# Two 8-expert mixtures in a six-stage transformer kernel: tiles of 128 rows, weights kept on chip, each tile's weights copied to a fixed place

## The chip, the cores and the metric

The kernel runs on one core of one Trainium2 chip. The metric is the device time of one launch in microseconds (us); lower is better. The program is written engine by engine: TensorE (PE), VectorE (DVE), ScalarE (ACT), GpSimd (POOL) and SyncE (SP), which only issues DMAs here, each have their own list of instructions, and semaphores order them against each other.

## What is computed

2048 tokens of 128 numbers pass through six stages, each with a residual: a 64-expert mixture, an attention, the 64-expert mixture again, an 8-expert mixture, a second attention, and the 8-expert mixture again. The change touches only the two 8-expert mixtures (called f1 and g1 in the code, their tensors `f_...` and `g_...`):

```python
x = x + 0.5 * _L1_ffn_ref(_layernorm(x, axis=-1), ...)   # stages 4 and 6

def _L1_ffn_ref(x, Wg, bg, W1, b1, W2, b2):      # 8 experts, 128 -> 512 -> 128
    probs = softmax(x @ Wg + bg, axis=-1)
    h = relu(einsum('bsd,edf->bsef', x, W1) + b1)
    all_out = einsum('bsef,efd->bsed', h, W2) + b2
    top_vals, top_idx = top_k(probs, 2)
    weights = top_vals / (sum(top_vals) + 1e-09)
    selected = take_along_axis(all_out, top_idx[..., None], axis=2)
    return sum(selected * weights[..., None], axis=2)
```

## The kernel before

The function `mixture_one` builds one such stage. All data are 32-bit floats. It has a **preamble** and a **tile loop**.

Preamble. VectorE computes the layer norm (L144 to L159), TensorE turns it (L165) and multiplies it by the gate (L369), and VectorE picks the two best experts of each token (L449 to L464) and computes, from ranks that TensorE sums (L376 to L382), the place of each of the 4096 (token, choice) pairs in a list sorted by expert (L469 to L484). In DRAM the list is `slots_dram`: it is cut into tiles of `SLOTS` = 256 rows, each tile of one expert alone, so there are at most `PASSES` = 16 + 7 = 23 tiles, and a row is 132 numbers (the token's vector and its number). SyncE fills the list with empty rows at the stage's start (L302). Once the places are known, GpSimd scatters the rows into it with 32 indirect DMAs (L352). The number of each tile's expert is put into `tile_expert` (L487 to L490).

Weights. SyncE loads them per tile: it reads the tile's expert into a register (`value_load`, L311) and issues four DMAs, W1 (256 KB), b1, W2 (256 KB) and b2 spread over all partitions (L312 to L315), into one of `WBUF` = 6 buffers. Six tiles' weights are loaded during the scatter, the others behind the loop as buffers come free. When all rows are scattered, four DMAs bring the list back to SBUF as `xin` (L321), in groups of tiles (0), (1 to 3), (4 to 11) and (12 to 22).

Tile loop. For tile i TensorE turns its rows (`turn`, L389, two transposes), VectorE copies the result out of PSUM (`xT_out`, L509), TensorE makes the 512 hidden values (`hidden`, L398, four matmuls of 256 columns), ScalarE adds b1 and applies relu (L434, four operations), TensorE multiplies by W2 (`down`, L407, eight matmuls of 128 columns), VectorE adds b2 (`y_out`, L516), and GpSimd scatters the tile's two halves to `back_dram` by token number (L358, two indirect DMAs). TensorE's order is written out by hand:

```python
        turn(0)
        for i in range(PASSES):
            if i + 1 < PASSES:
                turn(i + 1)
            hidden(i)
            if i >= 1:
                down(i - 1)
        down(PASSES - 1)
```

At the end SyncE waits for all of GpSimd's DMAs, loads `back` in four parts (L329), and VectorE adds each token's two rows, times their weights, to x (L531).

Of the kernel before, what the change touches and what calls it, by code (L numbers as in the profile page):

```python
# [22 lines left out]
P = 128  # L23
# [175 lines left out]
def mixture_one(core, name, ctx, w):  # L199

    nc = core.nc
# [28 lines left out]
    fill = sb("fill", [P, E1])  # L232
# [5 lines left out]
    tile_number = sb("tile_number", [1, PASSES])  # L238
    tile_cmp = sb("tile_cmp", [1, PASSES, E1])
    tile_sum = sb("tile_sum", [1, PASSES])  # L240
    tile_expert = sb("tile_expert", [1, PASSES], I32)
    place = sb("place", [P, TILES, E1])
# [10 lines left out]
    w1 = [sb(f"w1_{i}", [P, F1]) for i in range(WBUF)]  # L253
    w2 = [sb(f"w2_{i}", [P, FC1, P]) for i in range(WBUF)]
    b1 = [sb(f"b1_{i}", [P, FC1]) for i in range(WBUF)]
    b2 = [sb(f"b2_{i}", [P, P]) for i in range(WBUF)]
    xin = sb("xin", [P, PASSES * HALVES, ROW])
    xT = sb("xT", [P, 2, SLOTS])
    hT = sb("hT", [P, 2, FC1, SLOTS])
    y = [sb(f"y{i}", [P, HALVES, P]) for i in range(YBUF)]  # L260
# [25 lines left out]
    rows_sent, *y_sent = core.indirect([16 * K * TILES] + [16 * HALVES * len(range(s, PASSES, YBUF)) for s in range(YBUF)])  # L286
    w_loaded = [sem(f"w_loaded{i}") for i in range(WBUF)]
# [9 lines left out]
    def sync(sp):  # L297
# [6 lines left out]
        sp.wait_ge(experts_ready, 1)  # L304

        def weights(i):
            s = i % WBUF
            if i >= WBUF:
                sp.wait_ge(y_ready, i - WBUF + 1)
                sp.wait_ge(relu_done, FC1 * (i - WBUF + 1))  # L310
            e = sp.value_load(tile_expert[0:1, i:i + 1], min_val=0, max_val=E1 - 1)  # L311
            sp.dma_start(w1[s][:, :], w["W1"][ds(e, 1)].rearrange("a d f -> d (a f)")).then_inc(w_loaded[s], 16)  # L312
            sp.dma_start(b1[s][:, :], w["b1"][:, ds(e, 1), :].rearrange("p a c -> p (a c)")).then_inc(w_loaded[s], 16)
            sp.dma_start(w2[s][:, :, :], w["W2"][ds(e, 1)].rearrange("a (c p) d -> p (a c) d", p=P)).then_inc(w_loaded[s], 16)
            sp.dma_start(b2[s][:, :], w["b2"][ds(e, 1), :].to_broadcast([P, P])).then_inc(w_loaded[s], 16)  # L315

        for i in range(WBUF):
            weights(i)
        wait_sent(sp, rows_sent, 16 * K * TILES)
# [1786 lines left out]
```

## Time and profile before

| | us |
|---|---|
| median of 3 runs (1409.33 to 1413.65) | 1412.22 |
| the profiled execution's own time | 1405.89 |
| its span | 1404.2 |
| first 8-expert mixture, layer norm to the last addition to x | 672.5 to 853.4 |
| second 8-expert mixture, the same | 1217.3 to 1396.1 |
| TensorE busy over the span | 1006.7 (72%) |
| VectorE / ScalarE / GpSimd busy | 792.9 / 599.2 / 285.0 |

A span is the time from the first to the last instruction of the profiled execution. "Busy" leaves out register, branch and DMA-issuing instructions. A 32-bit matmul shows as two records on TensorE, a transpose as one, so `L398 PE ... x8` are the four matmuls of one tile. PEclk is the clock that TensorE was granted: 1.00 is 2.4 GHz and 0.50 is 1.2 GHz. The chain of waits is followed back from the last instruction, at each step to what released it.

### The profile page before, as it was taken

The numbers are of one execution on the slowest core, as the hardware profiler recorded it, in microseconds if no ns is written. First come the engines' busy times: TensorE is split into PE (matmuls) and PEld (weight loads), VectorE is DVE, ScalarE is ACT, GpSimd is POOL, SyncE is SP. The second block draws the span as 40 slices with busy tenths as digits, with TensorE's granted clock in tenths as the row PEclk, the third lists the DMA queues.
The fourth block names the chain that finished last, engine by engine and source line by source line (L and its number), as shares of the span: only waits on it lengthen the run. The fifth ranks groups of instructions, "written<-read, shape, count | busy, mean of one in ns | idle before, by whom it ended". The sixth has DMA issues, their size and how long they took to land.

```text
span 1404.2 us, 25630 instructions
## 1 busy us (share of the span) xinstructions
PE 1006.7 (72%) x8027; PEld 749.0 (53%) x8042; DVE 792.9 (56%) x2560; ACT 599.2 (43%) x1392; POOL 285.0 (20%) x321
## 2 busy tenths in 40 slices
PE   3798922488989667989307971789999999613992
PEld 2346822355656344568306971566676767412992
DVE  6766866756666577678501217377777776530222
ACT  3113613445666340147203431277777777411440
POOL 2103062321210030030073541000000000044552
PEclk8799967679999978999558995699999999855996
DMA  7003000000000060030456636855444443355652
GB/s 204 0 0 102 0 13 0 1 1 2 0 0 0 16 160 0 18 85 0 89 153 181 188 87 214 232 151 151 141 116 136 131 118 114 61 136 146 186 164 90
DMA packets 168677, 125.98 MB, mean 90 GB/s; under 512 B 16595, under 2 KB 151531, under 8 KB 168580
## 3 DMA queue, kind: packets, MB, share of 16 engines
q1 hardware_dynamic: 163588, 116.25, 30.7%
q0 software_dynamic: 4992, 8.54, 1.7%
q8 instruction: 48, 0.79, 0.2%
q14 instruction: 49, 0.40, 0.1%
HBM read 85.89 MB, written 40.69 MB: 90 GB/s over the span
## 4 chain that ended last, share of the span: by engine, by line
PE 56%; DVE 23%; issue 8%; ACT 5%; SPq 3%; DMA 2%; POOL 2%; POOLq 0%; DVEq 0%; ACTq 0%; PEld 0%; PEldq 0%
PE psum L398 6%; PE psum L407 6%; PE psum L746 5%; PE psum L831 4%; PE psum L1227 3%; PE psum L194 3%; PE psum L1779 3%; PE psum L1250 2%; PE psum L1791 2%; PE psum L1821 2%; PE psum L1284 2%; PE psum L1286 2%; PE psum L1215 2%; PE psum L1811 2%; PE psum L165 2%
## 5 line engine op out<-in xcount | busy, mean ns | idle before, releaser
L1460 DVE TENSOR_REDUCE a_negmax<-psum 128x2 f32<-128x512 f32 x128 | 88.4, 691 | 66.1 <-PE psum L1227 65.3
L1371 ACT ACTIVATE a_PT<-psum 128x1024 f32<-128x1024 f32 x64 | 65.5, 1024 | 78.0 <-PE psum L1286 78.0
L973 DVE TENSOR_TENSOR g_S<-g_place,g_number 128x512 bf16<-128x512 f32 (+1 forms) x116 | 76.8, 702 | 16.9 <-PEq L741 6.0
L434 ACT ACTIVATE g_hT<-psum,g_b 128x256 f32<-128x256 f32 x92 | 37.4, 471 | 97.8 <-PE psum L398 97.8
L434 ACT ACTIVATE f_hT<-psum,f_b 128x256 f32<-128x256 f32 x92 | 37.4, 471 | 97.5 <-PE psum L398 97.5
L973 DVE TENSOR_TENSOR f_S<-f_place,f_number 128x512 bf16<-128x512 f32 (+1 forms) x100 | 66.2, 704 | 16.3 <-PEq L741 6.1
L1896 ACT ACTIVATE a_pr<-a_L,a_least 128x128 f32<-128x128 f32 x128 | 50.7, 396 | 54.5 <-DVE a_least L1956 54.5
L1356 ACT ACTIVATE a_turned<-psum 128x1024 bf16<-128x1024 bf16 x64 | 64.4, 1021 | 8.4 <-PE psum L1215 8.4
L1227 PE MATMUL psum<-a_turned 128*128 128x256 bf16 x256 | 53.7, 295 | 13.8 <-DVE a_negmax L1460 11.1
L1898 ACT ACTIVATE a_pr<-a_L,a_least 128x256 f32<-128x256 f32 x128 | 63.5, 496 | 0.0
L1284 PE MATMUL psum<-a_turned 128*128 128x256 bf16 x256 | 60.7, 277 | 1.0 <-issue 0.5
L1286 PE MATMUL psum<-a_shift,a_select 128*128 128x256 bf16 x256 | 60.7, 277 | 0.0
L1779 PE MATMUL psum<-a_KT,a_Q 64*128 64x128 f32 (+1 forms) x512 | 59.3, 350 | 1.4 <-DVE a_least L1956 1.4
L1906 ACT ACTIVATE a_PT<-psum 128x384 f32<-128x384 f32 x128 | 55.8, 490 | 1.8 <-PE psum L1791 1.6
L1791 PE MATMUL psum<-ident,a_pr 128*128 128x128 f32 x384 | 53.6, 276 | 2.8 <-DVE a_pr L1717 2.5
L1811 PE MATMUL psum<-a_PT,a_V 128*64 128x256 f32 (+1 forms) x512 | 55.5, 338 | 0.0
L358 POOL DMA_INDIRECT g_back_dram<-g_y,g_xin x46 | 44.7, 972 | 53.1 <-DVE g_y L516 37.1
L358 POOL DMA_INDIRECT f_back_dram<-f_y,f_xin x46 | 44.7, 972 | 52.6 <-DVE f_y L516 37.9
L1956 DVE CUSTOM_DVE_ANT_0 a_L<-psum,a_X 128x256 f32<-128x256 f32 x128 | 53.6, 419 | 0.0
L1811 PEld LDWEIGHTS psum<-a_PT,a_V 128*64 128x64 f32 x512 | 31.0, 136 | 41.0 <-issue 16.8
L180 POOL CAST a_xs_high<-a_xnT 128x256 fp32r<-128x256 f32 x8 | 4.3, 539 | 231.9 <-PE psum L196 220.8
L1215 PE MATMUL psum<-identb,a_stack 128*128 128x128 bf16 x512 | 43.2, 236 | 10.4 <-ACT a_turned L1356 10.4
(472 smaller groups left out, 2749.2 us busy)
## 6 DMA issues: line engine op xcount, KB each, us to landing
a_z<-a_G SPq DMA_DIRECT2D x32, 512.0 KB, 3.9
a_X<-a_z SPq DMA_DIRECT2D x16, 1024.0 KB, 6.7
f_w<-in_W SPq DMA_DIRECT2D x46, 256.0 KB
g_w<-in_W SPq DMA_DIRECT2D x46, 256.0 KB
a_X<-a_z SPq DMA_DIRECT2D x16, 512.0 KB, 4.1
f_wgu<-in_gate_up SPq DMA_DIRECT2D x16, 384.0 KB, 6.5
g_wgu<-in_gate_up SPq DMA_DIRECT2D x16, 384.0 KB, 4.7
a_z<-a_pad SPq DMA_DIRECT2D x6, 1024.0 KB, 10.3
```

Of the source, the lines that this page charges most:

```text
L358: pool.indirect_dma_start(back_dram[:, :], bass.IndirectOffsetOnAxis(ap=xin[:, HALVES * i + a, P:P + 1].bitcast(I32), axis=0), y[i % YBUF] ...
L398: pe.matmul(bank[2 * (i % 2) + c // 2][:, SLOTS * (c % 2):SLOTS * (c % 2) + SLOTS], w1[i % WBUF][:, P * c:P * c + P], xT[:, i % 2, :], sta ...
L407: last = pe.matmul(bank[4 + i % 2][:, P * a:P * a + P], hT[:, i % 2, c, P * a:P * a + P], w2[i % WBUF][:, c, :], start=(c == 0), stop=(c = ...
L434: act.activation(hT[:, i % 2, c, :], bank[2 * (i % 2) + c // 2][:, SLOTS * (c % 2):SLOTS * (c % 2) + SLOTS], ACT.Relu, bias=b1[i % WBUF][: ...
L973: return dve.tensor_tensor(S[:, slot, :].rearrange("p (t e n) -> p t e n", t=1, n=CAPACITY), bcast(place[:, ds(t, 1), CE * k:CE * k + CE], ...
L1227: last = pe.matmul(bank[0][:, SEQ * j:SEQ * j + SEQ], turned[s][0][:, h + j, P * qt:P * qt + P], turned[s][1][:, h + j, :], start=True, st ...
L1284: pe.matmul(out[:, SEQ * j:SEQ * j + SEQ], turned[s][1][:, h, P * kt:P * kt + P], turned[s][0][:, h, :], start=True, stop=False, skip_grou ...
L1286: last = pe.matmul(out[:, SEQ * j:SEQ * j + SEQ], select[:, h, :], shift[s][:, :], start=False, stop=True, skip_group_check=True)
L1460: dve.tensor_reduce(negmax[:, qt, h:h + 2], bank[0].rearrange("p (h n) -> p h n", n=SEQ), AX.X, ALU.max, negate=True).then_inc(max_done, 1)
L1779: last = pe.matmul(out, Q[s][rows, c, queries], KT[s][rows, c, keys], start=True, stop=True)
L1791: last = pe.transpose(bank[2 + i][:, P * j:P * j + P], pr[:, n % SLOTS, P * j:P * j + P], core.ident[:, :])
L1811: last = pe.matmul(o[D1 * i:D1 * i + D1, queries], V[s][:, kt, D1 * h:D1 * h + D1], PT[:, (2 * m + i) % TSLOTS, keys], start=(kt == 0), st ...
```

## The change

Tiles have 128 rows (`SLOTS = P`), so there are 32 + 7 = 39 of them. All experts' W1 and W2 are loaded once, at the stage's start, right behind the empty rows, into `w12`; before each tile VectorE copies the tile's 128x1024 weights, at an address in a register, into one of three fixed places `wt` (`take_weights`). The 39 registers are loaded by VectorE ahead of the loop. b1 is picked for all tiles ahead of the loop (`tile_bias`), and b2 is no longer added to y: TensorE multiplies the tokens' expert weights `ex` by b2 ahead of the loop, and VectorE adds the product to x. In front of the loop TensorE also does 18 matmuls of 512 columns whose result nobody reads (`WARM`), once 28 of the 32 scatters have landed. The first two tiles' rows now come in one DMA. The diff, cut to its core (both mixtures run this code):

```diff
-    SLOTS = 256
-    HALVES = SLOTS // P
+    SLOTS = P
     PASSES = K * TOKENS // SLOTS + E1 - 1
-    WBUF = 6
-    YBUF = 4
-    GROUPS = ((0, 1), (1, 4), (4, 12), (12, PASSES))
+    YBUF = 6
+    WBUF = 3
+    GROUPS = ((0, 2), (2, 8), (8, 22), (22, PASSES))
+    LAST = 4
+    WARM = 18
...
     def sync(sp):
...
-        sp.wait_ge(experts_ready, 1)
-        def weights(i):
...
-        for i in range(WBUF):
-            weights(i)
-        wait_sent(sp, rows_sent, 16 * K * TILES)
+        sp.dma_start(b1[:, :, :], w["b1"]).then_inc(w_loaded, 16)
+        sp.dma_start(b2[:, :], w["b2"]).then_inc(w_loaded, 16)
+        for e in range(E1):
+            sp.dma_start(w12[:, e, 0:F1], w["W1"][e]).then_inc(w_loaded, 16)
+            sp.dma_start(w12[:, e, F1:2 * F1].rearrange("p (c d) -> p c d", d=P),
+                         w["W2"][e].rearrange("(c p) d -> p c d", p=P)).then_inc(w_loaded, 16)
+        wait_sent(sp, rows_sent, 16 * (K * TILES - LAST))
+        wait_sent(sp, last_sent, 16 * LAST)
...
     def gpsimd(pool):
...
         for i in range(PASSES):
             pool.wait_ge(y_ready, i + 1)
-            for a in range(HALVES):
-                pool.indirect_dma_start(back_dram[:, :],
...
+            pool.indirect_dma_start(back_dram[:, :],
...
     def tensor(pe):
...
+        pe.wait_ge(weights_ready, 1)
+        for t in range(TILES):
+            last = pe.transpose(bank[t // 4][0:E1, P * (t % 4):P * (t % 4) + P], ex[:, t, :], core.ident[:, :])
...
+        pe.wait_ge(w_loaded, 16 * (2 + 2 * E1))
+        for q in range(4):
+            pe.wait_ge(exT_ready, q + 1)
+            for t in range(4 * q, 4 * q + 4):
+                last = pe.matmul(bank[q][:, P * (t % 4):P * (t % 4) + P], exT[:, P * t:P * t + P], b2[:, :], start=True,
+                                 stop=True)
+            last.then_inc(b2_done, 1)
+        wait_sent(pe, rows_sent, 16 * (K * TILES - LAST))
+        for i in range(WARM):
+            pe.matmul(bank[4], core.ones[:, :], sel_flat, start=True, stop=True)
...
         def hidden(i):
-            pe.wait_ge(w_loaded[i % WBUF], 64 * (i // WBUF + 1))
             pe.wait_ge(xT_ready, i + 1)
+            pe.wait_ge(copied, i + 1)
...
         def down(i):
             if i >= 2:
                 pe.wait_ge(y_ready, i - 1)
-            pe.wait_ge(relu_done, FC1 * (i + 1))
-            for a in range(HALVES):
-                for c in range(FC1):
...
+            for c in range(FC1):
+                pe.wait_ge(relu_done, FC1 * i + c + 1)
...
     def vector(dve):
...
+        dve.wait_ge(w_loaded, 16 * (2 + 2 * E1))
+        for c in range(FC1):
+            step(dve.tensor_tensor(tile_pick[:, :, :], tile_cmp[:, :, :],
+                                   b1[:, :, c].unsqueeze(1).to_broadcast([P, PASSES, E1]), ALU.mult))
+            ins = dve.tensor_reduce(tile_bias[:, c, :], tile_pick[:, :, :], AX.X, ALU.add)
...
+        for q in range(4):
+            dve.wait_ge(b2_done, q + 1)
+            xq = core.x[:, 4 * q:4 * q + 4, :]
+            dve.tensor_tensor(xq, xq, bank[q].rearrange("p (t d) -> p t d", d=P), ALU.add).then_inc(b2_added, 1)
+        dve.wait_ge(experts_ready, 1)
+        expert = [dve.value_load(tile_expert[0:1, i:i + 1], min_val=0, max_val=E1 - 1) for i in range(PASSES)]
...
+        def take_weights(i):
+            if i >= WBUF:
+                dve.wait_ge(y_done, i - WBUF + 1)
+            dve.tensor_copy(wt[i % WBUF][:, :], w12[:, ds(expert[i], 1), :].rearrange("p a n -> p (a n)")).then_inc(copied, 1)
+        for i in range(WBUF):
+            take_weights(i)
         xT_out(0)
         for i in range(PASSES):
             if i + 1 < PASSES:
                 xT_out(i + 1)
+            if i >= 1 and i - 1 + WBUF < PASSES:
+                take_weights(i - 1 + WBUF)
             if i >= 1:
                 y_out(i - 1)
```

How the instructions stand before and after, at the places that matter most. TensorE in the tile loop of the first of the two mixtures, before (two tiles; `f_w_0` is a weight buffer, `f_xin` the rows, `f_xT` and `f_hT` the turned rows and the hidden values):

```order
L389 MATMUL psum<-ident,f_xin 128x128 x2
L398 MATMUL psum<-f_xT,f_w_1 128x256 x4
L407 MATMUL psum<-f_w_0,f_hT 128x128 x8
L389 MATMUL psum<-ident,f_xin 128x128 x2
L398 MATMUL psum<-f_xT,f_w_2 128x256 x4
```

and the same place in the changed kernel:

```order
L411 MATMUL psum<-f_sel,ones 128x512 x18
L417 MATMUL psum<-ident,f_xin 128x128 x2
L427 MATMUL psum<-f_xT,f_wt 128x128 x4
L417 MATMUL psum<-ident,f_xin 128x128
L427 MATMUL psum<-f_xT,f_wt 128x128 x4
L436 MATMUL psum<-f_wt,f_hT 128x128 x4
```

The 18 matmuls stand in front of the loop; a tile now has one transpose, four hidden matmuls of half the columns and four output matmuls in place of eight. VectorE in the same loop before:

```order
L503 TENSOR_REDUCE f_weight<-f_part 128x16
L509 COPY f_xT<-psum 128x256 x3
L516 TENSOR_TENSOR f_y<-psum,f_b_0 128x256
L509 COPY f_xT<-psum 128x256
L516 TENSOR_TENSOR f_y<-psum,f_b_1 128x256
```

and in the changed kernel (the first two rows are the last of 39 such pairs of rows, one for each register):

```order
L555 TENSOR_LOAD f_tile_expert
L555 ISA x2
L572 ISA
L572 COPY f_wt<-f_w 128x1024
L572 ISA
L572 COPY f_wt<-f_w 128x1024
L572 ISA
L572 COPY f_wt<-f_w 128x1024
L561 COPY f_xT<-psum 128x128 x3
L572 ISA
L572 COPY f_wt<-f_w 128x1024
L567 COPY f_y<-psum 128x128
```

Ahead of the first turned tile VectorE now has 39 register loads and three copies of weights, and between a tile's two PSUM copies it has one copy of 128x1024.

## Rows read from the trace of the kernel before

**Rows 1.** Windows inside both tile loops: length, busy time per engine, granted clock, DMA share, GB/s.
```profile
755.00:834.00 79.00, 79.00 (x554) 74.67 (x553) 16.23 (x42) 34.05 (x84) 40.84 (x42) 1.00 0.55 156
1297.00:1376.00 79.00, 79.00 (x554) 74.67 (x553) 16.42 (x42) 34.07 (x84) 40.84 (x42) 1.00 0.53 156
```

**Rows 2.** Chain that ended last, first two-choice mixture: start us, us, engine, output, line.
```profile
672.52 3.20 DVE f_moments L144 x16
...
743.49 3.65 DMA f_xin<-f_slots_dram
...
747.87 3.23 PE psum L398 x8
...
754.84 0.22 PE psum L389 x2
755.06 1.73 PE psum L398 x8
756.79 1.78 PE psum L407 x16
...
834.81 0.44 DVE f_y L516
...
838.05 2.08 DMA f_back_dram<-f_y,f_xin
840.28 3.71 DMA f_back<-f_back_dram
```

**Rows 3.** The same chain, second two-choice mixture.
```profile
1289.55 3.41 PE psum L398 x8
```

**Rows 4.** Timeline around the first tiles, all engines: start us, us, engine, line.
```profile
745.28 0.69 PE L389 MATMUL psum<-ident,f_xin 128*128 128x128 f32 x2 [48.18 <-DMA f_xin<-f_slots_dram]
...
754.88 0.42 DVE L516 TENSOR_TENSOR f_y<-psum,f_b 128x256 f32<-128x256 f32 x1 [3.09 <-PE psum L407]
...
756.08 0.97 POOL L358 DMA_INDIRECT f_back_dram<-f_y,f_xin  x1 [14.36 <-DVE f_y L516]
```

**Rows 5.** ScalarE groups, first mixture: busy us, mean ns, idle before.
```profile
L434 ACT ACTIVATE f_hT<-psum,f_b 128x256 f32<-128x256 f32 x92 | 37.4, 471 | 97.5 <-PE psum L398 97.5
```

**Rows 6.** DMA issues: KB each, median us to landing.
```profile
f_slots_dram<-f_empty SPq DMA_DIRECT2D x1, 3036.0 KB, 17.3
```

**Rows 7.** Windows in the first mixture: granted clock, DMA share, GB/s (last three columns).
```profile
680.00:684.00 4.00, 3.64 (x15) 2.70 (x15) 4.00 (x16) 1.59 (x3) 0.00 (x0) 0.50 1.24 211
720.00:724.00 4.00, 0.00 (x0) 0.00 (x0) 0.00 (x0) 0.00 (x0) 2.93 (x4) 0.50 0.37 121
```

**Rows 8.** GpSimd timeline, first and last scatter of the first mixture.
```profile
700.99 1.17 POOL L352 DMA_INDIRECT f_slots_dram<-f_rows,f_slot  x1 [27.23 <-DVE f_slot L484]
...
740.75 0.97 POOL L352 DMA_INDIRECT f_slots_dram<-f_rows,f_slot  x1 [0.30 <-issue]
```

**Rows 9.** VectorE queue instructions of one register load (ns min/median/max).
```profile
L969 DVEq FUSED_REGOPS  x2: 190/198/206, 55.0 to 535.3; - x2
...
L969 DVEq TENSOR_LOAD <-g_count x1: 316/316/316, 534.9 to 534.9; - x1
```

**Rows 10.** VectorE timeline, wide operations in the first attention.
```profile
209.24 1.42 DVE L1417 TENSOR_TENSOR a_z<-psum,a_bqkv 128x512 f32<-128x512 f32 x2 [4.92 <-PE psum L1318]
210.69 0.69 DVE L1419 TENSOR_SCALAR a_e<-a_z 128x1024 f32<-128x1024 f32 x1
...
225.96 1.31 DVE L1419 TENSOR_SCALAR a_e<-a_z 128x1024 f32<-128x1024 f32 x1
```

**Rows 11.** VectorE timeline, a 128x16 tensor_scalar beside GpSimd memsets.
```profile
184.87 2.59 DVE L150 TENSOR_SCALAR a_ve<-a_mean_var 128x16 f32<-128x16 f32 x1
```

**Rows 12.** GpSimd timeline at the same place.
```profile
180.47 6.96 POOL L1145 MEMSET a_stack<- 128x4096 bf16 x2 [47.33 <-SPq L2015]
```

**Rows 13.** VectorE timeline, the same shape beside a scatter.
```profile
1244.29 0.17 DVE L498 TENSOR_SCALAR g_den<-g_den 128x16 f32<-128x16 f32 x1
```

**Rows 14.** GpSimd timeline at that place.
```profile
1244.14 0.97 POOL L352 DMA_INDIRECT g_slots_dram<-g_rows,g_slot  x1 [0.30 <-issue]
```

More of the change, by code:

```diff
@@ L231, in mixture_one @@
     lower = sb("lower", [P, E1, E1])
-    fill = sb("fill", [P, E1])
+    FULL = TOKENS // SLOTS
+    fill = sb("fill", [P, FULL])
+    full = sb("full", [P, E1, FULL])
     cmp = sb("cmp", [P, E1, E1])
@@ L252, in mixture_one @@
     weight = sb("weight", [P, K, TILES])
[L253 to L257, printed above, removed]
+    w12 = sb("w12", [P, E1, 2 * F1])
+    wt = [sb(f"wt{i}", [P, 2 * F1]) for i in range(WBUF)]
+    b1 = sb("b1", [P, E1, FC1])
+    b2 = sb("b2", [E1, P])
+    exT = sb("exT", [E1, TOKENS])
+    xin = sb("xin", [P, PASSES, ROW])
     xT = sb("xT", [P, 2, SLOTS])
     hT = sb("hT", [P, 2, FC1, SLOTS])
-    y = [sb(f"y{i}", [P, HALVES, P]) for i in range(YBUF)]
+    y = [sb(f"y{i}", [P, P]) for i in range(YBUF)]
     back = sb("back", [P, TILES, K, P])
@@ L285, in mixture_one @@
     exp_done = sem("exp_done")
-    rows_sent, *y_sent = core.indirect([16 * K * TILES] + [16 * HALVES * len(range(s, PASSES, YBUF)) for s in range(YBUF)])
-    w_loaded = [sem(f"w_loaded{i}") for i in range(WBUF)]
+    rows_sent, last_sent, *y_sent = core.indirect([16 * (K * TILES - LAST), 16 * LAST] + [16 * len(range(s, PASSES, YBUF)) for s in range(YBUF)])
+    w_loaded = sem("w_loaded")
+    weights_ready = sem("weights_ready")
+    copied = sem("copied")
+    ex_turned = sem("ex_turned")
+    exT_ready = sem("exT_ready")
+    b2_done = sem("b2_done")
+    b2_added = sem("b2_added")
+    bias_ready = sem("bias_ready")
     x_loaded = [sem(f"x_loaded{i}") for i in range(len(GROUPS))]
@@ L403, in down @@
                 pe.wait_ge(y_ready, i - 1)
-            pe.wait_ge(relu_done, FC1 * (i + 1))
-            for a in range(HALVES):
-                for c in range(FC1):
-                    last = pe.matmul(bank[4 + i % 2][:, P * a:P * a + P], hT[:, i % 2, c, P * a:P * a + P],
-                                     w2[i % WBUF][:, c, :], start=(c == 0), stop=(c == FC1 - 1))
+            for c in range(FC1):
+                pe.wait_ge(relu_done, FC1 * i + c + 1)
+                last = pe.matmul(bank[4 + i % 2][:, 0:P], hT[:, i % 2, c, :],
+                                 wt[i % WBUF][:, F1 + P * c:F1 + P * c + P],
+                                 start=(c == 0), stop=(c == FC1 - 1))
             last.then_inc(y_done, 1)
@@ L525, in vector @@
         y_out(PASSES - 1)
+        dve.wait_ge(b2_added, 4)
         for q in range(4):
```

94 lines of the change are left out of this document (51 added, 43 removed).

## The prediction

> **What bounds the kernel now.** I read the windows of the two tile loops first. TensorE is busy for all 79.00 of 79.00 us in both, at the full clock, while VectorE has 16, ScalarE 34 and GpSimd 41 us of work [rows 1]. So inside the loops TensorE alone sets the end, and the DMA traffic of the per-tile weights (156 GB/s) costs nothing as long as it keeps up. The chain of waits then gives a tile's price: 0.22 for two transposes, 1.73 for four hidden matmuls of 256 columns, 1.78 for eight output matmuls of 128, 3.73 us in all [rows 2]. Ahead of the loop the chain runs through the layer norm, the routing and GpSimd's 32 scatters, which start 1.28 us apart from 700.99 to 740.75 [rows 8]; the weight loads stand beside them. After the scatters come one DMA (first transposes at 745.28, rows 4), then a wait for the second group's DMA, so that hidden starts only at 747.87 [rows 2]. The first tile's hidden matmuls take 3.23 and 3.41 us in place of 1.73 [rows 2, 3], since up to there the granted clock is 0.50, that is 1.2 GHz [rows 7].
>
> **The loop.** A 128-column matmul of this kind costs 1.78 / 8 = 0.223 us [rows 2], and the new hidden matmuls have just the shape of the output matmuls. A tile of 128 rows is then 0.11 + 4 x 0.223 + 4 x 0.223 = 1.89 us. Two of them cost 0.05 more than one old tile; the gain is that less is padded: 39 x 128 = 4992 rows in place of 23 x 256 = 5888. From the first transpose to the end of the last output matmul:
> - before: 834.81 - 745.28 = 89.5 us [rows 2, 4].
> - after: 0.9 for one transpose, the PSUM copy and their semaphores (the first two tiles come in one DMA, so the wait for a second group is gone), 39 x 2 x 0.89 = 69.4, 37 x 0.11 = 4.1 for the other transposes, 0.5 for the relus that the last tile can't hide: 74.9 us.
> - saved: 14.6 in the first mixture, and 0.2 more in the second [rows 3]: 29.4 us.
>
> This supposes the full clock from the first tile, by the 18 matmuls ahead of it. They start with the 28th scatter's landing, some 6 us before the rows are back, and need 18 x 512 columns, 7.7 us at 1.2 GHz and 3.8 at 2.4. They may come a little late or not raise the clock in time; that is worth 0 to 2 us per mixture (3.23 and 3.41 against 1.73, rows 2, 3), and I take 1 each: **-2.0**.
>
> What else must keep step with 1.89 us:
> - ScalarE: 37.4 / 92 = 0.41 us for a relu of 256 columns [rows 5]; four of 128 can't take more than 1.62.
> - GpSimd: one scatter per tile at 1.28, the same rows per scatter as now [rows 8].
> - VectorE: a PSUM copy of 128 columns is near 0.28 (0.42 for 256, rows 4; 0.71 for 512, rows 10). The 1024-wide weight copy has no row of its own; nearest is a one-input 128x1024 operation in SBUF, 0.69 us, and 1.31 when GpSimd was at work [rows 10]. From the end of output matmuls i-1 VectorE must do the copy, y and the next xT; TensorE needs that xT after one transpose, four hidden and four output matmuls and the next transpose, 2.0 us later. With 0.69 VectorE needs 1.4, with 1.31 2.0. So both ends cost about nothing, and I take 0; the copy stops being hidden past 1.3 us.
>
> **The end of the loop.** Before, 5.5 us pass from the last output matmul to the issue of the loads of back (834.81 to 840.28, rows 2): y, then queued scatters one after another. After, the last scatter can start 1.28 us behind the one before it. A scatter starts 0.78 us after its y (755.30 to 756.08, rows 4), so the last starts 1.3 us after the last output matmul, and it lands within 2.2 (838.05 to 840.28, rows 2): 3.6 us. Saved 1.9 twice: **3.8 us**.
>
> **Ahead of the loop.** The new work is meant to hide beneath the scatters. When do the weights land? The empty rows take 17.3 us for 5888 rows [rows 6], so 14.7 for 4992, from about 673.5 (the stage starts at 672.5, rows 2): 688.2. Then 4.19 MB of weights at 211 GB/s [rows 7]: 19.9 us, to 708. From there:
> - VectorE picks b1 with 8 operations of 312 elements, 0.5 each: 4.0 us. Beside it TensorE does 16 matmuls for b2 at the low clock, 3.23 / 8 = 0.40 each: 6.5 us. The last addition of 128x512 is 0.71 [rows 10]: 7.2 us after the landing.
> - 39 register loads. VectorE's queue shows one: load 0.316, register arithmetic 0.198 [rows 9], and I add 0.15 for the check and the gaps: 0.66 each, 25.7 us. This is the largest new piece.
> - three weight copies: 2.1 us.
>
> That ends 35.0 us after the landing, at 743.1; the first xT is wanted at 745.7. In the first mixture 2.6 us are to spare. In the second the rows come back 3 us sooner after the stage's start, so it is 0.4 late. With twice 0.15 for two wider comparisons ahead of the scatters I charge **-1.0 us**. The cover is the scatters' 41 us; without it the whole chain would show. The b2 product costs nothing beside it, and y no longer needs b2.
>
> **The sum.** 29.4 - 2.0 + 3.8 - 1.0 = 30.2 us. Against the profiled execution's own 1405.9 that is 1375.7. The median of the three runs is 6.3 us above that execution, so against it: **1382.0 us**. This kernel's measurement can tell some 0.3% (4 us) from no change.
>
> **Rivals.**
>
> *Late weights or registers (1388 to 1408; 1396 as its middle).* At 720 to 724, beside the scatters, the queues together moved only 121 GB/s, though SyncE had loads to issue; the scatters' share is 67.6 KB per 1.28 us, 53, which leaves 68 [rows 7, 8]. Of the weights 2.7 MB would be there at 701; if the rest came at 68 GB/s, it would take 22 us, to 723, and the loops would start 12 and 15 us late: 1410. Halfway, 1396. Register loads at 0.8 us add 5.5 us to each mixture as well. Against: the loads are issued early, and most go before the scatters begin.
>
> *A longer tile by the SBUF port (1386 to 1396; 1394).* If each scatter stands still for the length of a copy, GpSimd needs 1.28 + 0.69 = 1.97 us per tile: 3 us per mixture. If the copy waits a little as well, a tile of 2.05 us gives 39 x 0.16 = 6.2 us twice, 1394.
>
> *Slower: the copy waits for the end of every scatter (1451).* In this rhythm a scatter runs from 0.78 to 1.75 us after its y, and the next copy wants to start 0.9 us after that y, inside it. If it must wait, the tile's cycle becomes 0.78 + 0.97 for the scatter, 0.69 for the copy, 0.28 for y and 0.05: 2.77 us in place of 1.89. 39 x 0.88 = 34.3 us per mixture: 1382 + 69 = 1451. It decides as soon as the cycle passes 2.0. For it: a one-input VectorE operation of 128x16 took 2.59 us while memsets ran on GpSimd [rows 11, 12], and the 1024-wide one 1.31 instead of 0.69 [rows 10]. Against it: an operation of the same 128x16 shape started 0.15 us into a scatter and took 0.17, and the scatter kept its 0.97 [rows 13, 14]. So the scatter seems not to hold the port as a memset does, at least at its start.
>
> The Trainium skill (SBUF — State Buffer, Who interferes with whom) states that such a VectorE operation and a GpSimd instruction exclude each other for the whole instruction, whichever comes second being blocked; by that rule the 1451 is what to expect. The memset rows agree with it, the row beside the scatter does not.
>
> *Not doing what it says:* fewer padded rows and one scatter less per two tiles follow from the sizes alone; only the clock part can fail, and it is in the sum by half.
>
> **Chances.** The forecast (all of 1376 to 1389) 0.58, late weights or registers 0.20, the longer tile 0.12, the exclusive port 0.07; 0.03 is left for what no row shows. Faster by over 0.3% (below 1408): 0.58 + 0.12 + nine tenths of the 0.20 = 0.88. Within 0.3%: 0.03. Slower: 0.07 + 0.02 = 0.09. The range takes in the forecast and most of the first two rivals, 1375 to 1401 us, and leaves out the exclusive port and the worst of the late starts.
>
> **What would show it.** Right: four hidden matmuls in 0.89 us, 1.89 from tile to tile, TensorE busy throughout the loop, the clock at 1.00 at the first tile; VectorE's last register load and third copy before the rows are back; weight copies of 0.69 to 1.31. Wrong: VectorE, not a DMA, as releaser of the first hidden matmuls (late start), copies of over 1.3 us or scatters of over 1.3 (port), a tile period of 2 us and more with TensorE idle in it.

## The result and the profile after

| | before | after | ratio |
|---|---|---|---|
| median of 7 runs, us | 1412.2 (1409.3 to 1413.7) | 1422.1 (1416.2 to 1424.6) | 1.0065 [1.0043, 1.0087] |
| span of the profiled execution, us | 1404.2 | 1420.3 | |
| first mixture: start to start of the next stage, us | 183.8 | 187.4 | |
| attention between the two, us | 361.0 | 360.3 | |
| second mixture to the end of the span, us | 186.9 | 194.4 | |

The change made the kernel slower by 10 us, where 30 us less was forecast. (Of the 16.1 us between the spans, 11.1 lie in the two mixtures and 5.8 in the untouched stages ahead of them.) That figure is not the whole truth of this kernel: the same file, run again, took 1378.2 us in one set of runs, 1386.2 in a single run of another, and 1422.7 to 1428.4 in three others (medians). The experiments tell how.

TensorE in the first mixture after the change, from its timeline (start us, us, engine, line, operation, in brackets the idle time before and what ended it); it answers to [rows 2, 4]:
```profile
744.10 6.82 PE L411 MATMUL psum<-f_sel,ones 128*128 128x512 bf16 x18 [27.12 <-DMA f_slots_dram<-f_rows,f_slot]
751.51 0.44 PE L417 MATMUL psum<-ident,f_xin 128*128 128x128 f32 x2 [0.59 <-DMA f_xin<-f_slots_dram]
769.88 2.07 PE L427 MATMUL psum<-f_xT,f_wt 128*128 128x128 f32 x8 [17.94 <-DVE f_xT L561]
...
773.64 1.06 PE L436 MATMUL psum<-f_wt,f_hT 128*128 128x128 f32 x8
774.54 0.27 PE L417 MATMUL psum<-ident,f_xin 128*128 128x128 f32 x1
774.65 1.06 PE L427 MATMUL psum<-f_xT,f_wt 128*128 128x128 f32 x8
775.54 1.06 PE L436 MATMUL psum<-f_wt,f_hT 128*128 128x128 f32 x8
```
The rows are back on time: the first transposes come 73.2 us after the stage's start (678.28), before 72.8. Then TensorE stands idle for 17.94 us, and VectorE is what ends it. From there a tile takes 1.89 us (773.64 to 775.54, with rounding), as forecast, and in the windows inside the loops TensorE is busy all the time at the full clock, VectorE 0.58 of it (columns as in [rows 1]):
```profile
780.00:840.00 60.00, 60.00 (x540) 59.92 (x539) 34.60 (x94) 36.19 (x127) 33.16 (x32) 1.00 0.10 33
1330.00:1388.00 58.00, 58.00 (x522) 58.00 (x521) 33.41 (x93) 34.89 (x123) 31.73 (x31) 1.00 0.10 34
```
The loop's end is as forecast too: last y at 845.78, loads of back issued at 849.42, 3.64 us. What VectorE did in the 17.94 us are the register loads. Its queue instructions of that line, with the ns of one as min/median/max and the first and last start:
```profile
L555 DVEq FUSED_REGOPS  x78: 2/183/709, 723.7 to 1316.1; - x78
L555 DVEq SEQ_ASSERT  x78: 4/23/709, 723.9 to 1316.3; - x78
L555 DVEq TENSOR_LOAD <-f_tile_expert x39: 11/299/709, 723.3 to 767.0; - x39
```
The medians are close to those of [rows 9], a load in 0.61 us, but single ones take 709 ns. In the trace the first loads come 0.61 us apart until 727.5; from then to 752 each queue instruction takes a step of 0.70 us, three to six steps a load; then they come at 0.61 again. 39 loads last 44 us, not 25.7. In the second mixture the additions of b2, ahead of the loads, are late, shown here in the chain that ended last:
```profile
1257.58 5.05 PE psum L404 x32
1262.66 0.69 DVE x L552
1263.35 3.52 another core or an unknown queue
1266.89 0.69 DVE x L552
1267.58 6.40 issue
1273.98 0.69 DVE x L552
1274.66 14.71 issue
1289.37 0.33 DVE x L552
```
TensorE's products for b2 had ended, yet the additions came 3.5, 6.4 and 14.7 us apart. The loads could begin at 1289.4 only, when the scatters were nearly over, took 27 us and ended 21 us behind the rows (turned at 1295.6).

What the additions waited for is TensorE's semaphore, which it raises after every four of its 16 products (eight records each time). The changed kernel's trace in set 2 shows it at the same place, where all four of these updates are recorded; here is its chain that ended last, cut to 1272 to 1301 us (TensorE's last product ends at 1265.2):
```profile
1272.74 0.02 issue
1272.76 0.69 DVE x L552
1273.45 9.19 another core or an unknown queue
1282.64 0.02 issue
1282.66 0.69 DVE x L552
1283.35 16.83 another core or an unknown queue
1300.18 0.02 issue
1300.21 0.33 DVE x L552
```
The updates stand at 1266.38, 1272.74, 1282.64 and 1300.18, and each addition starts 0.02 to 0.03 us behind its own. So the last update came 35 us behind the product that it tells of. In the result's first mixture the last two came at 719.75 and 723.29, up to 6.3 us late; in set 5 below, where nothing is slow, all four came within 0.02 us of the product's end.

**One more thing in this trace.** It holds 9,155 semaphore updates, that of the same file in set 5 holds 11,037. Of the 1,882 that it lacks, 1,766 are landings of DMAs (4,058 recorded, 5,824 in set 5). VectorE's and ScalarE's stand, where they are recorded, within 0.02 us of their instruction's end; from 707.9 us on, as the scatters start, single ones are missing. They are missing in the tile loops too, beside the scatters of y (of ScalarE's four a tile, one in nearly every tile), and nowhere outside the two 8-expert mixtures. In the loops the queue instructions take their usual time (TENSOR_LOAD 0.30 to 0.32 us in set 3, in the version that has loads there). So a gap in the record doesn't by itself mean a slow queue.

### The profile page after: what moved, and what is told of

Its sections match the earlier page's. It is cut to its first block, busy times and chain, and to the rows that moved or that the text cites. A ratio compares the mean times of both kernels' runs of the same rounds, so it can differ in the third digit from the quotient of the medians.

```text
span 1420.3 us, 26307 instructions
## 1 busy us (share of the span) xinstructions
PE 1018.4 (72%) x8304; PEld 756.2 (53%) x8304; DVE 859.3 (61%) x2730; ACT 618.5 (44%) x1528; POOL 276.8 (19%) x309
## 4 chain that ended last, share of the span: by engine, by line
PE 54%; DVE 24%; issue 9%; ACT 4%; DVEq 4%; POOL 2%; DMA 1%; another core or an unknown queue 1%; SPq 0%; POOLq 0%; ACTq 0%; PEld 0%; PEldq 0%
PE psum L806 5%; PE psum L427 5%; PE psum L436 5%; PE psum L891 4%; DVEq L555 3%; PE psum L1287 3%; PE psum L194 3%; PE psum L1839 3%; PE psum L1310 2%; PE psum L1851 2%; PE psum L1344 2%; PE psum L1881 2%; PE psum L1346 2%; PE psum L1275 2%; PE psum L1871 2%
## 5 line engine op out<-in xcount | busy, mean ns | idle before, releaser
L465 ACT ACTIVATE g_hT<-psum,g_tile_bias 128x128 f32<-128x128 f32 x156 | 44.7, 368 | 91.3 <-PE psum L427 91.3
L465 ACT ACTIVATE f_hT<-psum,f_tile_bias 128x128 f32<-128x128 f32 x156 | 44.6, 369 | 87.4 <-PE psum L427 87.4
L1033 DVE TENSOR_TENSOR f_S<-f_place,f_number 128x512 bf16<-128x512 f32 (+1 forms) x100 | 66.2, 703 | 15.4 <-PEq L801 6.2
L572 DVE COPY f_wt<-f_w 128x1024 f32 x39 | 27.1, 699 | 74.2 <-issue 43.7
L1287 PE MATMUL psum<-a_turned 128*128 128x256 bf16 x256 | 54.6, 298 | 13.0 <-DVE a_negmax L1520 10.1
L1344 PE MATMUL psum<-a_turned 128*128 128x256 bf16 x256 | 63.0, 284 | 0.8 <-DVE a_shift L1535 0.5
L572 DVE COPY g_wt<-g_w 128x1024 f32 x39 | 26.9, 694 | 57.4 <-PE psum L436 31.0
L427 PE MATMUL psum<-g_xT,g_wt 128*128 128x128 f32 x312 | 43.1, 283 | 22.6 <-DVE g_xT L561 22.6
L427 PE MATMUL psum<-f_xT,f_wt 128*128 128x128 f32 x312 | 43.1, 283 | 17.9 <-DVE f_xT L561 17.9
L367 POOL DMA_INDIRECT g_back_dram<-g_y,g_xin x39 | 40.4, 1035 | 64.9 <-DVE g_y L567 63.6
```

The lines of the kernel that those rows point to most:

```text
L427: last = pe.matmul(bank[i % 2][:, P * c:P * c + P], wt[i % WBUF][:, P * c:P * c + P], xT[:, i % 2, :], start=True, stop=True)
L465: act.activation(hT[:, i % 2, c, :], bank[i % 2][:, P * c:P * c + P], ACT.Relu, bias=tile_bias[:, c, i:i + 1]).then_inc(relu_done, 1)
L1033: return dve.tensor_tensor(S[:, slot, :].rearrange("p (t e n) -> p t e n", t=1, n=CAPACITY), bcast(place[:, ds(t, 1), CE * k:CE * k + CE], ...
L1287: last = pe.matmul(bank[0][:, SEQ * j:SEQ * j + SEQ], turned[s][0][:, h + j, P * qt:P * qt + P], turned[s][1][:, h + j, :], start=True, st ...
L1344: pe.matmul(out[:, SEQ * j:SEQ * j + SEQ], turned[s][1][:, h, P * kt:P * kt + P], turned[s][0][:, h, :], start=True, stop=False, skip_grou ...
```

## The experiments

Eighteen kernels, some of them the same file again, ran in six sets; the kernels of a set ran one after another on one chip. Theory A: the loads, beside the scatters, cost the time. Its rivals: the loads cost nothing and something else holds the loop's start; later, theory C, that the slow steps belong to a set and not to a kernel. (The expectations name their theories set by set: C is another theory in the first set, the one on the sets is called R in the second, and "call" in them is a set.) Sets 1 to 6 ran on chips 0, 15, 15, 3, 2 and 3. The whole at a glance, "updates" being the semaphore updates that the kernel's trace holds:

| set | kernel | us | updates | slow steps |
|---|---|---|---|---|
| result | before / after | 1412.2 / 1422.1 | 9,728 / 9,155 | yes |
| 1 | load with each tile | 1382.9 | 11,037 | no |
| 1 | scatters held back | 1453.9 | 11,038 | no |
| 1 | loads first | 1376.6 | 11,038 | no |
| 1 | before + 39 loads | 1411.4 | 13,350 | no |
| 2 | changed kernel | 1428.4 | 9,122 | yes |
| 2 | kernel before | 1413.6 | 9,838 | yes |
| 2 | 20 loads first, 19 later | 1414.0 | 9,117 | yes |
| 2 | no filling products | 1427.5 | 9,146 | yes |
| 3 | changed kernel | 1423.8 | 9,137 | yes |
| 3 | load with each tile | 1383.0 | 9,118 | yes |
| 3 | loads first | 1415.5 | 9,217 | yes |
| 3 | copies ahead of additions | 1380.2 | 9,133 | yes |
| 4 | changed kernel | 1422.7 | 9,121 | yes |
| 4 | copies ahead, no filling | 1384.4 | 9,229 | yes |
| 5 | changed kernel | 1378.2 | 11,037 | no |
| 5 | spaced scatters | 1475.8 | 11,101 | no |
| 6 | changed kernel | 1386.2 | 11,037 | no |
| 6 | spaced scatters | 1470.2 | 11,099 | no |

The kernel before, timed in every set, had medians of 1412.1 to 1413.6.

### A load with each tile (sets 1 and 3)
```diff
-        expert = [dve.value_load(tile_expert[0:1, i:i + 1], min_val=0, max_val=E1 - 1) for i in range(PASSES)]
         def take_weights(i):
+            e = dve.value_load(tile_expert[0:1, i:i + 1], min_val=0, max_val=E1 - 1)
...
```


> The changed kernel with each register loaded just ahead of its own tile's weight copy, so that 3 loads stand before the loop in place of 39. Theory A (the 39 loads ahead of the loop, slowed while GpSimd scatters back to back, are the whole loss): the first hidden matmuls of the first mixture start about 74 us after the stage's first bn_stats in place of 91.6, those of the second about 71 in place of 92.8, a tile stays at 1.89 us since a load of 0.61 fits into VectorE's 0.8 us of idle time, and the whole takes 1382 to 1388 us. Theory B (VectorE's queue is slow beside any scatter, also one per tile): a tile grows to 2.5 us or more and the time does not fall below that of the changed kernel.

Measured: 1382.9 us, 0.976 [0.973, 0.980] of before. A load of 0.61 fits into VectorE's idle time of each tile. I read from it that the loads in a block were the loss; but this set had no slow steps, and where there are none the block costs nothing either (set 5).

### Scatters held back until the copies are made (set 1)
```diff
         pool.wait_ge(slots_ready, 2)
+        pool.wait_ge(copied, WBUF)
```


> The changed kernel with GpSimd's 32 scatters held back until VectorE has made its 39 loads and three weight copies. Theory A (back-to-back scatters slow VectorE's queue): each load takes 0.61 us, the 39 take 24 us in both mixtures, and the additions of b2 to x run without gaps. Theory C (a long chain of register loads slows itself, or the queue's instructions arrive late, whatever GpSimd does): 44 us for the 39 loads with steps of 0.70 us as in the changed kernel. The time grows by some 30 us per mixture either way, since the scatters start later.

Measured: 1453.9 us in one run; scatters from 745.3 to 785.1, loads 0.61 each. This agreed with theory A, and so misled: in this set nothing was slow, scatters or not.

### All loads first (sets 1 and 3)
```diff
         dve.tensor_copy(tile_expert[:, :], tile_sum[0:1, :]).then_inc(experts_ready, 1)
+        dve.wait_ge(experts_ready, 1)
+        expert = [dve.value_load(tile_expert[0:1, i:i + 1], min_val=0, max_val=E1 - 1) for i in range(PASSES)]
...
-        dve.wait_ge(experts_ready, 1)
-        expert = [dve.value_load(tile_expert[0:1, i:i + 1], min_val=0, max_val=E1 - 1) for i in range(PASSES)]
```


> The changed kernel with the 39 loads moved up, right behind the tile table, ahead of the expert weights, b1 and b2. They then begin within 1 us of the first scatter. Theory A with an onset some time into the scatters (20 us in the first mixture): 30 or more loads at 0.61 us each, 18 to 24 us in all, then the slow steps hit what is left: the b1 selection and the additions. VectorE is through in time or at most 10 us late: 1385 to 1405 us. Theory C: the loads take 44 us again, and the time stays within 5 us of the changed kernel's.

Measured: 1376.6 us, 0.973 [0.968, 0.977]. The scatters ran from 707.1 to 747.2, and all 39 loads beside them at 0.63 each:
```profile
L524 DVEq TENSOR_LOAD <-f_tile_expert x39: 297/304/369, 707.6 to 731.7; - x39
L524 DVEq TENSOR_LOAD <-g_tile_expert x39: 297/303/366, 1232.9 to 1256.7; - x39
```
So that loads run beside scatters isn't enough. Theory A's mechanism fell, its place stood.

### 39 loads in the kernel before (set 1)
```diff
+        dve.wait_ge(experts_ready, 1)
+        for j in range(39):
+            dve.value_load(tile_expert[0:1, j % PASSES:j % PASSES + 1], min_val=0, max_val=E1 - 1)
```


> The kernel before, with 39 unused register loads on VectorE ahead of its tile loop (the other parts of the change undone). My forecast's price, 0.66 us each, would end them at 731, and the time would not change. Theory A: they are slowed in the second half of the scatters, end some 3 to 10 us after the rows are back, and cost 3 to 10 us per mixture. If the time does not change, the slowing needs another part of the change.

Measured: 1411.4 us, 0.999 [0.996, 1.001], loads at 0.63 each. More telling is SyncE's queue, which issues four loads a tile there. In the kernel before, in the trace shown ahead of the prediction:
```profile
716.68 0.01 SPq L312 DMA_DIRECT2D f_w<-in_W  x1
718.11 0.70 SPq L313 DMA_DIRECT2D f_b<-in_b  x1
720.21 0.70 SPq L314 DMA_DIRECT2D f_w<-in_W  x1
722.30 0.70 SPq L315 DMA_DIRECT2D f_b<-in_b  x1
727.24 0.71 SPq L312 DMA_DIRECT2D f_w<-in_W  x1
```
and in this one:
```profile
715.82 0.34 SPq L312 DMA_DIRECT2D f_w<-in_W  x1
716.34 0.33 SPq L313 DMA_DIRECT2D f_b<-in_b  x1
716.77 0.39 SPq L314 DMA_DIRECT2D f_w<-in_W  x1
717.34 0.51 SPq L315 DMA_DIRECT2D f_b<-in_b  x1
718.61 0.34 SPq L312 DMA_DIRECT2D f_w<-in_W  x1
```
A tile's four issues took up to 10.6 us in the first (716.68 to 727.24) and 2.8 us in the second. The queues moved 121 GB/s at 720 to 724 us in the first and 322 in the second. Adding loads to VectorE can't have sped up SyncE. Here theory C came from.

### Both kernels once more (set 2)


> The changed kernel once more, unchanged. What is asked is whether the stretches in which VectorE's and SyncE's queues move in steps of 0.70 us (727.5 to 752.0 us in the profile of the changed kernel, 711 to 734 us on SyncE in that of the kernel before) belong to the kernel. Theory A (they belong to it: register loads behind the additions, beside the scatters): the same again, 1422 us, 44 us for the 39 loads in the first mixture, gaps of some 25 us between the second mixture's additions. Theory R (they belong to the execution or to its recording: in that profile the recorded semaphore updates of VectorE and TensorE come later and later behind the instructions from 708 us on, and from 712 us on most are missing; the profiles of the experiments so far have no such stretch): the loads take 39 x 0.61 = 24 us, they end at about 743, the first hidden product follows the rows (752 instead of 770, 1297 instead of 1319), and the time is about 1422 - 17.6 - 21.9 = 1383 us.

> The kernel before once more, unchanged, one look. Theory A: SyncE's queue moves in steps of 0.70 us from 711 to 734 us again. Theory R: SyncE's weights for the first tiles are issued at about 2.7 us each throughout, as in the kernel before with 39 loads added, and no semaphore updates are missing. Under both the time is 1409 to 1414 us, since SyncE's queue isn't waited for there.

Measured: 1428.4 us, 1.012 [1.009, 1.015], loads 42 us; and 1413.6 us, SyncE's queue slow again. Taken alone this spoke for theory A, or for anything that belongs to the kernel.

### 20 loads first, 19 at their place (set 2)
```diff
+        expert = [dve.value_load(tile_expert[0:1, i:i + 1], min_val=0, max_val=E1 - 1) for i in range(20)]
...
-        dve.wait_ge(experts_ready, 1)
-        expert = [dve.value_load(tile_expert[0:1, i:i + 1], min_val=0, max_val=E1 - 1) for i in range(PASSES)]
+        expert += [dve.value_load(tile_expert[0:1, i:i + 1], min_val=0, max_val=E1 - 1) for i in range(20, PASSES)]
```


> 20 of the 39 register loads right behind the table of the tiles' experts, 19 where the change has them. Theory A: the last 19 come slow where the scatters run (0.61 to 2.1 us each), and the b2 additions have gaps. 20 loads end at about 719.5 us; selection of b1 and additions until about 733 us; then 19 loads: by 0.61 each until 745 (time as with all loads first, 1377 us), by 2.1 each until about 758 (1385 us or more). Theory R: 1377 us, no slow step.

Measured: 1414.0 us, 1.001 [0.999, 1.002], far above theory R's 1377 and also above the 1385 "or more" of theory A. The first 20 loads ran at 0.61 each, to 721. But TensorE was late as well. Of its 16 products for b2 (32 records) the last four came 8.4 us behind the others, and its four semaphore updates all came between 753.40 and 753.68, 10.6 us behind the last product and 5.4 behind the start of the last scatter; only then could the additions start:
```profile
726.78 5.52 PE L404 MATMUL psum<-f_b,f_exT 8*128 8x128 f32 x24
740.73 2.07 PE L404 MATMUL psum<-f_b,f_exT 8*128 8x128 f32 x8 [8.43 <-issue]
```
```profile
753.42 2.48 DVE L554 TENSOR_TENSOR x<-x,psum 128x512 f32<-128x512 f32 x4 [22.74 <-remote]
765.82 1.90 DVE L573 COPY f_wt<-f_w 128x1024 f32 x3 [9.92 <-issue]
```

### TensorE without its wait and its filling products (set 2)
```diff
-        wait_sent(pe, rows_sent, 16 * (K * TILES - LAST))
-        for i in range(WARM):
-            pe.matmul(bank[4], core.ones[:, :], sel_flat, start=True, stop=True)
```


> The changed kernel without TensorE's wait for the rows and without the 18 filling products behind it (nothing that is computed hangs on them). It prices them, and shows whether a TensorE that waits there has to do with the slow steps. Theory A: 1422 us, or some 20 to 40 us less if TensorE's wait is part of the cause. Theory R: the clock at the head of the tile loops is lower than with the products; at the low clock TensorE's 0.89 us for four products become 1.78, and the first tiles take about 1.8 us more each for some tiles: 2 to 12 us more than the unchanged kernel in the same call, since the loads keep TensorE idle anyway for most of the time between.

Measured: 1427.5 us, 1.011 [1.008, 1.013], as the changed kernel of this set (1428.4): a TensorE that waits for the scatters is no part of the cause, and the products are worth nothing when TensorE idles 18 us behind them.

### The changed kernel beside its two better versions (set 3)


> The changed kernel, unchanged, now in one call on one chip with the two kernels that took its loads out of the way. So far the slow steps showed in every kernel of two calls (the kernel before and the changed one in the first, and all four kernels of the third, the kernel before among them) and in no kernel of the second. Theory K (the kernel decides): 1422 to 1428 us, loads of the first mixture 42 to 44 us, second mixture's additions 25 us or more apart, while the two others of this call show no slow step. Theory C (the chip or the recording of a call decides, whatever the kernel): all kernels of this call show the slow steps, or none does; if none, this one comes to about 1383 us by the 17.6 and 21.9 us that the first hidden products come earlier.

> The first experiment (each tile's register load just ahead of its copy) once more. Theory K: 1383 us, no gaps between the b2 additions. Theory C, if the slow steps show in this call: the b2 additions end only when the scatters do (at about 756 us, as in the kernel with 20 and 19 loads), three loads and copies follow, and the first hidden product comes at about 760 instead of 754 us: 1383 + 2 x 5 = 1393 us.

> All 39 loads right behind the table once more. Theory K: 1377 us. Theory C, with slow steps: the loads end at 732 as long as they come at 0.61 us each, the additions wait for the scatters' end, copies behind them: first hidden product at about 758: 1377 + 2 x 4 = 1385 us, more if the loads themselves are slowed.

Measured: 1423.8 us (1.008 [1.006, 1.011]), 1383.0 us (0.981 [0.978, 0.984]) and 1415.5 us (1.003 [1.001, 1.005]). The third settles it: the very file that took 1376.6 us in set 1 takes 1415.5 here, with no overlap (1373 to 1379, 1410 to 1422). Its loads:
```profile
L524 DVEq TENSOR_LOAD <-f_tile_expert x39: 1/304/700, 708.5 to 751.6; - x39
L524 DVEq TENSOR_LOAD <-g_tile_expert x39: 3/300/700, 1247.9 to 1292.8; - x39
```
The slow stretch begins at 725 us and ends with the scatters; its start isn't tied to a place in the code. All four traces of the set show it. The version with a load for each tile is as fast as in set 1: its last addition started at 720.8 us in the first mixture and at 1272.9 in the second, where the rows were turned at 1273.5, and only three loads and copies stood behind it; the first hidden product came 2.6 us after the first transpose there, against 0.7 in the first mixture.

### Copies ahead of the additions (set 3), and this without the filling products (set 4)
```diff
         ins.then_inc(bias_ready, 1)
+        dve.wait_ge(experts_ready, 1)
+        for i in range(WBUF):
+            take_weights(i)
         for q in range(4):
             dve.wait_ge(b2_done, q + 1)
```
with each tile's load ahead of its copy, as above.

> Each tile's load just ahead of its copy, and the first three loads and copies ahead of the b2 additions. If no slow step shows: as the lazy kernel, 1383 us (the additions end well ahead of the rows either way). If they show: only the additions are left behind the scatters' end, the first hidden product waits for the first of them alone (about 754 us, with the rows): 1383 us again, 10 us below the lazy kernel of the same call.

> The kernel with its first copies ahead of the additions (1380.2 us), without TensorE's wait for the rows and the 18 filling products behind it. If they bring the clock up for the tile loop: the first tiles run at the low clock, the four products of a tile taking 1.78 us instead of 0.89, in both mixtures; 4 to 12 us more than 1380. If the clock comes up as late with them as without: 1380.

Measured: 1380.2 us, 0.978 [0.975, 0.980], in a set with slow steps: better than both kernels, and the lowest median there, though the load with each tile has single runs just as low (1379.3); not 10 us below it, as forecast, but 2.8, since that version hadn't come to 1393 but to 1383.0. Without the filling products 1384.4 us, 0.979 [0.976, 0.983]. The difference of 4 us lies across two sets, and the runs overlap (1379.7 to 1380.6 with them, 1378.5 to 1385.8 without), so that the medians alone don't show it. The loops do, in part: from first transpose to last y 75.0 and 75.0 us with the products, 76.6 and 76.9 without. But sets 5 and 6 have loops of 76.4 to 76.6 with them too: what they bring is 0 to 2 us a mixture.

### The changed kernel in three more sets (sets 4 to 6)


> The changed kernel once more. If this call shows the slow steps: 1417 to 1430 us, loads of the first mixture 42 to 44 us. If it doesn't: loads 24 us in both mixtures, no gaps between the additions, first hidden product with the rows, about 1383 us.

> The changed kernel once more. With the slow steps: 1417 to 1430 us. Without: loads 24 us in both mixtures, first hidden product with the rows, about 1383 us.

> The changed kernel, one look, as the measure of its call: 1417 to 1432 us and loads of 42 to 44 us in the first mixture if the call has the slow steps, 1378 us and 24 us if not.

Measured: 1422.7 us (1.008 [1.005, 1.012]) in set 4, with slow steps and 44 us of loads; **1378.2 us (1377.5 to 1379.8), 0.976 [0.975, 0.978]**, in set 5 and 1386.2 us in one run in set 6, both without. (The 8 us between these two lie in all parts of the kernel: 3.4 ahead of the first mixture, 3.1 in the two mixtures, 2.2 in the attention between.) Sets 4 and 6 ran on the same chip, so the chip alone doesn't decide. The queue instructions and TensorE's timeline in set 5:
```profile
L555 DVEq FUSED_REGOPS  x78: 183/183/190, 714.7 to 1264.9; - x78
L555 DVEq SEQ_ASSERT  x78: 23/23/23, 714.9 to 1265.1; - x78
L555 DVEq TENSOR_LOAD <-f_tile_expert x39: 297/310/359, 714.3 to 738.7; - x39
```
```profile
741.60 6.68 PE L411 MATMUL psum<-f_sel,ones 128*128 128x512 bf16 x18 [27.35 <-DMA f_slots_dram<-f_rows,f_slot]
749.21 0.44 PE L417 MATMUL psum<-ident,f_xin 128*128 128x128 f32 x2 [0.93 <-DMA f_xin<-f_slots_dram]
749.92 1.16 PE L427 MATMUL psum<-f_xT,f_wt 128*128 128x128 f32 x8 [0.27 <-DVE f_xT L561]
```
and VectorE's, without a gap between the additions and with the copies 8 us ahead of the rows:
```profile
713.97 2.47 DVE L552 TENSOR_TENSOR x<-x,psum 128x512 f32<-128x512 f32 x4
739.40 1.90 DVE L572 COPY f_wt<-f_w 128x1024 f32 x3 [22.96 <-issue]
749.58 0.49 DVE L561 COPY f_xT<-psum 128x128 f32<-128x128 f32 x2 [8.28 <-PE psum L417]
```

### Scatters at half their rate (sets 5 and 6)
```diff
                                         oob_is_err=False).then_inc(...)
+                pool.memset(pace[:, :], 0.0).then_inc(paced, 1)
+                pool.wait_ge(paced, k * TILES + t + 1)
```


> The changed kernel with a memset of 128x1024 on GpSimd behind each scatter, waited for: one scatter in about 2.5 us instead of 1.28. The rows are back some 40 us later in each mixture, so that the time, 1450 to 1500 us, says nothing; what is read is the pace of VectorE's queue beside the scatters. If their rate makes it slow (and the call shows slow steps at all, see c5_after): 39 loads in 24 us, no gaps between the additions. If it is enough that scatters run: loads at 0.70 us and more per queue instruction again, until the scatters end.

> The kernel with a scatter every 2.66 us instead of 1.28, one look, about 1476 us whatever the call. If the call has the slow steps and their cause is the rate of the scatters: loads in 24 us, additions without gaps, all semaphore updates recorded (some 11,100). If their cause is only that scatters run: slow queue and additions until the scatters end, updates missing. If the call has no slow steps: as before, and the question stays open.

Measured: 1475.8 and 1470.2 us. Both sets were without slow steps, so whether the scatters' rate brings them about stays open.

## Why the prediction was wrong

**The step that failed** is the one on the 39 register loads ("0.66 each, 25.7 us", hidden by "the scatters' 41 us"), and with it "The b2 product costs nothing beside it". Where no queue is slow, it holds: 25.0 us in set 5, 0.64 each. In the result's own executions the cover was itself the trouble: while the scatters ran, queue instructions took steps of 0.70 us, so that 39 loads took 44 us in the first mixture, and in the second TensorE's semaphore updates for b2 came so late that the last addition ahead of the loads started 26.7 us after the first. Forecast was a spare of 2.6 us in the first mixture and a lack of 0.4 in the second; TensorE stood idle before its first hidden product for 17.9 and 22.6 us. These 40.5 us are more than the 30.2 that were to be gained.

**The trace of before had shown it.** SyncE's queue in the kernel before moved in the same steps beside the scatters (its rows above). I read its small throughput, 121 GB/s [rows 7], "though SyncE had loads to issue", as slow transfers, and made of it a rival in which weights land late. The weights landed 30.0 us after the stage's start (708.3), forecast 35.5, since they moved at over 300 GB/s from 696 us on. It was the issuing queue that was slow beside the scatters, and VectorE's and TensorE's were hit like SyncE's. The rival named the right place, "late weights or registers", and a load at 0.8 us; its end, 1408, was 14 us short.

The other steps, by set 5 for the forecast's own case and by the result's trace for the rest:
- **The loop.** From the first transpose to the last y: forecast 74.9 us; 824.13 - 749.21 = 74.9 in set 5. In the result's trace 94.3, 17.9 of them idle at the start.
- **The clock** (1 us a mixture): in set 5 the first tile's four hidden matmuls took 1.16 us in the first mixture, and those of the first two tiles 1.40 and 1.92 in the second, against 1.06 at the full clock; the loops took 74.9 and 76.4 us, so that it cost about 0 and 1.5. In the second the granted clock was 1.00 at 1270 to 1276 us and 0.50 again at 1276 to 1278; TensorE had stood idle for 2.66 us ahead of the first transposes, in the first mixture for 0.93. In the result's trace the idle time came between the filling products and the loop, and the hidden matmuls of the first two tiles took 2.07 and 1.85 in the first mixture: the products bought nothing.
- **The end of the loop**: forecast 3.6 us, 3.64 and 3.66 (824.13 to 827.79).
- **Ahead of the loop**: forecast was that the third copy ends 70.6 us after the stage's start. In set 5 it ended after 65.8 (741.3), thanks to the earlier weights; in the result's trace after 91.3 (769.6). The rows come 0.9 us later than before in set 5; forecast 0.3.
- **The sum** for both mixtures was -30.2 us. In set 5 they take 168.4 and 172.2 us, -15.4 and -14.7 against before: -30.1. The median there is 1378.2, forecast 1382.0. Between the medians lie 33.9 us, so 3.8 of them are outside the two mixtures and no part of the forecast. (One sentence of the prediction is wrong without harm: two new tiles need two scatters like one old tile; in all there are 39 for 46.)

**The port.** The copy of 128x1024 took 0.69 us in the loop, beside a scatter or not, and a scatter 1.04 instead of 0.97:
```profile
L572 DVE COPY f_wt<-f_w x39: 685/694/908, 767.7 to 841.3; 128x1024 f32 x39
```
```profile
L367 POOL DMA_INDIRECT f_back_dram<-f_y,f_xin x39: 967/1042/1207, 776.5 to 847.2; - x39
```
The 68 copies that ran wholly or mostly beside a scatter took 0.694 us on average, the 8 beside none 0.690, and two that touched one's edge 0.80. The longer tile (1394) and the exclusive port (1451) both fell. The rule of the Trainium skill by which the 1451 was to be expected (SBUF — State Buffer, Who interferes with whom) is not borne out for a copy beside these scatters: nobody is blocked for a whole instruction. The selection of b1, with two inputs in SBUF, took 0.71 us where a comparison of the same size took 0.48, but that is its own price: it took 0.72 too where the scatters were held back and none ran.

**What stays open** is the cause of the slow steps. Shown is: they come and go by the set, not by the kernel (8 kernels with none, 10 and the two of the result with them), and chip 3 had a set with and a set without; they hit the queue instructions of VectorE and SyncE and the products and semaphore updates of TensorE; they begin some 10 to 21 us behind the start of the first scatter and are over at the latest 6 us behind the start of the last; in each of these executions some 1,900 of the changed kernel's 11,037 recorded updates are missing (the kernel before kept 9,728 and 9,838, with 39 loads added, which raise no semaphore, 13,350), and in none of the others. The expectations of set 2 say that VectorE's updates trail ever more; that came from counting past missing ones. Which is cause and which effect the runs don't tell: a recorder that falls behind and holds the engines back, or something else on the chip that slows both. Every run here has a recorded span and clock, and no experiment leaves the recording out, so it is not known either whether the changed kernel is slow when nothing is recorded. The Trainium skill (NOTIFIC — the notification-queue block, Overflow: three behaviours, one of which stalls the engine) states that the block which writes such records pushes back on its producers rather than lose a record inside it, and so can throttle an engine; no run here shows that this is what happens.

## What to carry to other kernels

A work item that is "hidden" beside a busy stretch is hidden only at the rate that its queue has in that stretch: look in the trace at how fast any queue moves there, even one for which nobody waits. Keep small queue work (register loads, waits) out of a block on the critical engine, and spread it over the loop where that engine has idle time: the version with a load for each tile took 1383 us with and without the slow steps, the versions with the block of loads 1377 to 1386 without and 1414 to 1428 with them. And where two kernels are compared, run both in the same set before believing in a mechanism: the first experiments here seemed to explain the loss only because their set had no slow steps.

## What was not expected

- A register load (TENSOR_LOAD 0.30, FUSED_REGOPS 0.18, SEQ_ASSERT 0.02, and gaps) takes 0.61 us; forecast 0.66. The Trainium skill (DMA: Bandwidth & Descriptors, Latency and other measured facts) gives a floor of about 600 ns for `tensor_load`; the trace agrees if the whole load is meant, while the instruction TENSOR_LOAD alone takes 0.30 us.
- TensorE's semaphore updates came up to 35 us behind their products in sets with slow steps, and within 0.02 us in set 5.
- One file took 1378 us in one set and 1423 in another, each tight in itself (1377.5 to 1379.8; 1420.6 to 1425.8), while the kernel before stayed at 1412 to 1414 in all: its slow queue was there too, but off the path.
